# Three edits in one kernel: a copy moved from ScalarE to VectorE in the scan, a stencil by corner sums, softplus by its rounding

## The chip, the cores and the metric

The kernel runs on one core of a Trainium2 chip. The engines of a core run beside each other: TensorE (PE in the profile), VectorE (DVE), ScalarE (ACT), GpSimd (POOL), and SyncE (SP), which issues DMAs. The metric is the device time of one execution in microseconds (us). The kernel before takes 13669.76 us, the median of 3 runs (13667.76 to 13674.38).

## The reference, cut to what matters

The input is `[2, 192, 96, 96]` in float32. Four blocks are added to it in turn, each behind a group norm. Block 1 (two deformable convolutions) and block 3 are not touched. Of blocks 2 and 4 this matters:

```
# block 2: x is the normalised input
lap   = [[0, -1, 0], [-1, 4, -1], [0, -1, 0]]
edges = conv(x, lap)                      # depthwise, padding 1
out   = x + edges                         # 5 x - (up + down + left + right)
y     = conv1x1(out, merge_w) + merge_b   # 192 to 192 channels, then added to the stream

# block 4: tokens t = 0..9215 per image, 384 inner channels, 16 states
delta = softplus(dt_lin + b_dt)
def step(h, inp):
    u_t, d_t, B_t, C_t = inp
    dA = exp(d_t[..., None] * A)
    h = dA * h + (d_t * u_t)[..., None] * B_t[:, None, :]
    y_t = einsum('bdn,bn->bd', h, C_t)
```

## The kernel before, in words

The program is a chain of eight phases, each with its own tiles and semaphores and each closed before the next starts. Three are touched.

**edges_and_merge** (8821.4 to 9144 us of the span) loads an image of 96 x 9216 x 2 halves in four quarters into `X1`. ScalarE writes the normalised image with a border of zeros into `XP` (L963). The image goes through in 48 chunks of 4 rows (384 pixels). For each, GpSimd adds up and down into `T1` (L980) and left and right into `T2` (L981), VectorE adds the two (L1019) and makes `E` = 5 x - sum (L1022), TensorE multiplies by the weights (L992, 4 matmuls in float32, two records each), and VectorE adds bias and residual (L1007) and takes statistics for the next norm (L1012, `bn_stats`). SyncE stores the chunk. The second image is loaded only when the first is through.

**mamba_inputs** (10296 to 11022 us) has 36 steps of 512 tokens. TensorE makes the inner projections in `PX` and `PZ`; ScalarE copies `PX` to `XH` (`fill`, L1681), takes silu, and of the step size v it makes relu(v), |v| and `EE` = exp(-|v|) (L1707 to L1713), and then ln(1 + `EE`) (L1719). VectorE makes the depthwise convolution (L1783, L1788), copies `PD` (L1829), and in `small` and `whole` finishes softplus: below 2^-7 a polynomial of third degree stands for ln(1 + e) (L1798 to L1815).

**mamba_scan** (11022 to 13664 us) has 36 chunks of 512 tokens and 16 states n each, which makes 576 steps i; 384 channels lie on 128 partitions in three groups d. A step runs over four engines:
- ScalarE writes `BU`, four scaled copies of 128x384 (L1960), one for each 128 tokens `tb`, with the scale read from the tile, then three exponentials of 128x512 into `DA` (L1967). It also copies the carry of an earlier step (L1943).
- TensorE transposes `BU` into `PB` in PSUM (`turn`, L2014, once for each d), and adds G of two steps earlier to `PY` by an identity matmul (`accumulate`, L2024).
- VectorE runs `scan(i, d)` (L2072): `tensor_tensor_scan` over 512 tokens, with `DA` in SBUF and `PB` in PSUM as inputs, `HH` in SBUF as output.
- GpSimd multiplies `HH` of the step by row C (`CB`, spread over the partitions by a DMA) into `G`, 128x1536 in one instruction (L1988), once `scan(i, 2)` has ended.

Once a chunk, at n = 2, VectorE does `skip_path` (L2077) and `gate` (L2082) for each d; at n = 4 to 9 TensorE does `project` (L2032), at n = 10 VectorE `put` (L2090) and GpSimd `gain` (L1977); at n = 11 and 12 TensorE does `turn_gain`. `BU`, `DA`, `HH` and `G` have three buffers each. `PB` has one for each d, so that `turn(i + 1, d)` waits for `scan(i, d)`.

The order on each engine is as written in the code; nothing else sets it. `p.tick` is a 1x1 memset that raises a semaphore.

Of the kernel before, what the change touches and what calls it, by code (L numbers as in the profile page):

```python
# [8 lines left out]
ACT = mybir.ActivationFunctionType  # L9
# [4 lines left out]
HW = H * W  # L14
# [9 lines left out]
NEAR1 = 2.0 ** -7  # L24
HC = C // 2
# [872 lines left out]
def edges_and_merge(nc, k):  # L898

    RC = 4  # L900
    NP = RC * W
    NCH = H // RC
    WP = W + 2
    with Phase(nc, "ed") as p:
        GN = p.sb([HC, 4, 2])
        group_norm_terms(nc, k, k.ST, NCH, GN)
        X1 = p.sb([HC, 2, HW])
        XP = p.sb([HC, 2, (H + 2) * WP])
        T1 = p.sb([HC, 2, 2, NP])
        T2 = p.sb([HC, 2, 2, NP])  # L910
        E = p.sb([HC, 2, 2, NP])
        XO = p.sb([HC, 2, 2, NP])
        WM = p.sb([HC, 2, C])
        BM = p.sb([HC, 2])
        PE = [p.ps([HC, 2, 512]) for _ in range(2)]
        s_w, s_v, s_z, s_xn, s_t, s_e, s_pe, s_xo, s_bf, s_tf, s_x1f = p.sems(11)
        s_wr = p.sems(2)
        s_x1 = p.sems(4)
        s_st = p.sems(2)
        QR = H // 4  # L920
        XPv = XP[:, :, :].rearrange("p h (y x) -> p h y x", x=WP)
        chunks = [(c // NCH, c % NCH) for c in range(B * NCH)]

        def at(r, dy, dx, h):
            return XPv[:, h, r * RC + 1 + dy:r * RC + 1 + dy + RC, 1 + dx:1 + dx + W]

        def tile(T, q, h):
            return T[:, q, h, :].rearrange("p (y x) -> p y x", x=W)

        with p.block() as blk:  # L930
            @blk.sync
            def _(e):
                e.dma_start(WM[:, :, :], k.d["w_mergeT"].rearrange("(h p) o -> p h o", p=HC)).then_inc(s_w, 16)
                e.dma_start(BM[:, :], k.d["b_mergeT"]).then_inc(s_w, 16)
                e.wait_ge(s_w, 32).then_inc(s_w, -32)
                for s in s_wr:
                    e.sem_inc(s, 1)
                for b in range(B):
                    if b:
                        e.wait_ge(s_x1f, 1).then_inc(s_x1f, -1)  # L940
                    for i in range(4):
                        n0, n1 = i * QR * W, (i + 1) * QR * W
                        e.dma_start(X1[:, :, n0:n1], k.d["x1"][b, :, :, n0:n1].rearrange("h p n -> p h n"))\
                            .then_inc(s_x1[i], 16)
                    for r in range(NCH):
                        c = b * NCH + r
                        q = c % 2
                        e.wait_ge(s_xo, 1).then_inc(s_xo, -1)
                        e.dma_start(k.d["x2"][b, :, :, r * NP:(r + 1) * NP].rearrange("h p n -> p h n"), XO[:, q, :, :])\
                            .then_inc(s_st[q], 16)  # L950
                for q in range(2):
                    e.wait_ge(s_st[q], 16).then_inc(s_st[q], -16)
# [14 lines left out]

            @blk.gpsimd
            def _(e):
                e.memset(XP[:, :, :], 0.0).then_inc(s_z, 1)  # L970
                for c, (b, r) in enumerate(chunks):
                    q = c % 2
                    if r == 0:
                        e.wait_ge(s_xn, 2).then_inc(s_xn, -2)
                    elif r % (NCH // 4) == NCH // 4 - 1 and r < NCH - 1:
                        e.wait_ge(s_xn, 2).then_inc(s_xn, -2)
                    if c >= 2:
                        e.wait_ge(s_tf, 1).then_inc(s_tf, -1)
                    for h in range(2):
                        e.tensor_tensor(tile(T1, q, h), at(r, -1, 0, h), at(r, 1, 0, h), ALU.add)  # L980
                        ins = e.tensor_tensor(tile(T2, q, h), at(r, 0, -1, h), at(r, 0, 1, h), ALU.add)  # L981
                    ins.then_inc(s_t, 1)

            @blk.tensor
            def _(e):
                e.wait_ge(s_wr[0], 1).then_inc(s_wr[0], -1)
                for c in range(len(chunks)):
                    q = c % 2
                    e.wait_ge(s_e, 1).then_inc(s_e, -1)
# [588 lines left out]
NS = 16  # L1578
# [637 lines left out]
```

## Time and profile before

| | |
|---|---|
| median of 3 runs | 13669.76 us |
| profiled execution | 13666.01 us |
| its span | 13664.2 us |
| granted TensorE clock, mean | 0.954 |
| TensorE busy | 12753.0 us (93%) |
| VectorE busy | 11814.1 us (86%) |
| ScalarE busy | 11116.3 us (81%) |
| GpSimd busy | 7173.1 us (52%) |

The span runs from the first to the last recorded instruction; the profiled execution took 1.8 us more. Times in the rows are microseconds from the span's start, and L12 is a line of the kernel before. An engine's busy time says how much it worked, not that others waited for it; that is told by the brackets of a row of the timeline, `[0.88 <-PE ms_p L2024]`: the engine stood idle for 0.88 us ahead of this instruction, until line 2024 on TensorE was done. `DVEq` stands for the engine's own queue, where a wait on a semaphore is held. PEclk is the granted TensorE clock in tenths: 1.00 is 2.4 GHz, 0.50 is 1.2 GHz. `x9` is a row of nine instructions of one form, back to back.

### The profile page before, as it was taken

The page shows a single profiled execution, that of the slowest core. Times are in us where ns is not written, and L with a number is a line of the kernel's source. Part 1 is how long each engine was busy: PE and PEld are TensorE (multiplying, and loading weights), DVE is VectorE, ACT ScalarE, POOL GpSimd, SP SyncE. Part 2 cuts the span into 40 slices and gives each one's busy share as a digit, 9 for nine tenths or more (in the row PEclk, how much of TensorE's full clock was granted, in tenths as well). Part 3 has the DMA queues.
Part 4 walks back from the last instruction along what each step waited for, and adds up shares of the span by engine and source line. Part 5 has one row for each costly group of instructions (what it writes and reads, how often), then busy time and mean ns, then how long its engine had stood idle before and what let it go on. Part 6 is the DMA issues. An engine that isn't in the chain of part 4 may idle for free. (4 is left out here: it accounts for less than half of the span.)

```text
span 13664.2 us, 237197 instructions
## 1 busy us (share of the span) xinstructions
PE 12753.0 (93%) x80318; PEld 10364.2 (76%) x80318; DVE 11814.1 (86%) x15792; ACT 11116.3 (81%) x13034; POOL 7173.1 (52%) x3803
## 2 busy tenths in 40 slices
PE   7899999999999999999999999866098989999999
PEld 4799999999999999999999999322033345555555
DVE  4699999999999999999999999579867978888888
ACT  2688888888888888888888888219676878998898
POOL 0255555555555555555555555143320058888887
PEclk9999999999999999999999999578598889999999
DMA  4677767667777766767776666734443433333332
GB/s 124 161 178 179 178 178 177 177 177 178 178 179 178 177 177 177 179 177 178 179 177 177 178 177 169 187 82 165 132 133 119 151 116 106 103 105 99 105 103 85
DMA packets 826538, 2102.27 MB, mean 154 GB/s; under 512 B 83476, under 2 KB 440266, under 8 KB 681802
## 3 DMA queue, kind: packets, MB, share of 16 engines
q1 hardware_dynamic: 760994, 2046.19, 56.4%
q10 hardware_dynamic: 64359, 40.89, 1.1%
q8 instruction: 669, 10.96, 0.4%
q14 instruction: 516, 4.22, 0.1%
HBM read 1818.10 MB, written 268.74 MB: 153 GB/s over the span
## 5 line engine op out<-in xcount | busy, mean ns | idle before, releaser
L513 PE MATMUL dc_p<-dc_t 96*128 96x144 f32 x51948 | 6846.2, 285 | 25.8 <-PEq L510 25.8
L579 POOL TENSOR_TENSOR dc_t<-dc_t 128x648 f32<-128x648 f32 x2885 | 4526.3, 1569 | 4016.6 <-POOLq L578 3970.1
L513 PEld LDWEIGHTS dc_p<-dc_t 96*128 96x128 f32 x51948 | 6529.7, 189 | 47.0 <-issue 26.3
L639 DVE TENSOR_TENSOR dc_t<-dc_p,dc_t 128x1296 f32<-128x1296 f32 x2886 | 4343.7, 1505 | 507.3 <-DVEq L637 444.6
L458 ACT ACTIVATE dc_t<-dc_t 96x1152 f32<-96x1152 f32 x2892 | 3590.2, 1241 | 464.0 <-ACTq L482 457.4
L460 ACT ACTIVATE dc_t<-dc_t 96x1152 f32<-96x1152 f32 x2892 | 3367.7, 1164 | 347.2 <-ACTq L459 10.1
L2072 DVE TENSOR_TENSOR_SCAN ms_t<-ms_t,ms_p 128x512 f32<-128x512 f32 x1728 | 2128.4, 1271 | 283.3 <-PE ms_p L2014 203.5
L1988 POOL TENSOR_TENSOR ms_t<-ms_t 128x1536 f32<-128x1536 f32 x576 | 1987.9, 3456 | 503.3 <-DVE ms_t L2072 499.5
L2024 PE MATMUL ms_p<-ms_t,top_t 128*128 128x512 f32 x3456 | 1774.7, 596 | 0.0
L553 PE MATMUL dc_p<-dc_t 128*128 128x180 f32 (+1 forms) x7488 | 1633.6, 318 | 14.7 <-PEq L548 8.7
L2014 PEld LDWEIGHTS ms_p<-top_t,ms_t 128*128 128x128 f32 x6912 | 848.7, 141 | 968.6 <-issue 692.1
L651 DVE TENSOR_TENSOR dc_t<-dc_t 128x648 f32<-128x648 f32 x1442 | 1196.0, 829 | 211.8 <-DVEq L649 197.2
L1960 ACT ACTIVATE ms_t<-ms_t 128x384 f32<-128x384 f32 x2304 | 1222.2, 602 | 24.2 <-PE ms_p L2014 24.1
L553 PEld LDWEIGHTS dc_p<-dc_t 128*128 128x128 f32 (+1 forms) x7488 | 1162.1, 190 | 40.9 <-issue 34.4
L1967 ACT ACTIVATE ms_t<-ms_t 128x512 f32<-128x512 f32 x1728 | 1114.1, 708 | 0.0
L2014 PE MATMUL ms_p<-top_t,ms_t 128*128 128x128 f32 x6912 | 1047.1, 274 | 58.5 <-DVE ms_t L2072 51.6
L629 DVE COPY dc_t<-dc_p 128x128 f32<-128x128 f32 (+1 forms) x3744 | 978.4, 280 | 0.0
L542 PE MATMUL dc_p<-top_t,dc_t 128*128 128x128 f32 (+1 forms) x3744 | 877.8, 272 | 0.5 <-PEq L539 0.5
L659 DVE TENSOR_TENSOR dc_t<-dc_t 128x324 f32<-128x324 f32 x1441 | 703.6, 488 | 0.0
L1977 POOL TENSOR_TENSOR ms_t<-ms_t 128x1536 f32<-128x1536 f32 x36 | 124.6, 3461 | 812.5 <-DMA ms_t<-bcd 812.5
L2024 PEld LDWEIGHTS ms_p<-ms_t,top_t 128*128 128x128 f32 x3456 | 522.2, 191 | 15.8 <-DVE ms_t L2082 11.5
L542 PEld LDWEIGHTS dc_p<-top_t,dc_t 128*128 128x128 f32 (+1 forms) x3744 | 516.9, 138 | 11.9 <-issue 0.7
(209 smaller groups left out, 9823.8 us busy)
## 6 DMA issues: line engine op xcount, KB each, us to landing
dc_t<-sxd SPq DMA_DIRECT2D x1446, 864.0 KB, 5.7
ms_t<-bcd SPq DMA_DIRECT2D x576, 256.0 KB, 3.3
dc_t<-xrT SPq DMA_DIRECT2D x145, 675.0 KB, 8.3
kvd<-wk_t SPq DMA_DIRECT2D x18, 1536.0 KB, 5.1
xvd<-mi_t SPq DMA_DIRECT2D x36, 768.0 KB, 3.5
szd<-mi_t SPq DMA_DIRECT2D x36, 768.0 KB, 5.7
dld<-mi_t SPq DMA_DIRECT2D x36, 768.0 KB, 3.4
ms_t<-dld SPq DMA_DIRECT2D x36, 768.0 KB, 6.8
```

The source lines that it names most:

```text
L458: e.activation(HX[:, q, u, :], HX[:, q, u, :], ACT.Abs, bias=QX[:, 0:1]).then_inc(s_ab, 1)
L460: e.activation(HX[:, q, u, :], HX[:, q, u, :], ACT.Relu, bias=1.0, scale=-1.0).then_inc(s_hx, 1)
L513: ins = e.matmul(PT[j % 2][:, t // 3, (t % 3) * 144:(t % 3 + 1) * 144], HX[:, m // 2 % RP, m % 2, t * 128:(t + 1) * 128], XW[:, i, ky:ky + ...
L542: ins = e.transpose(PR[0:o, u * 128:(u + 1) * 128], VA[:, n // NG % 2, 128 * c:128 * c + o], k.ident[:, :])
L553: ins = e.matmul(PF[:, conv * CM:(conv + 1) * CM], VT[0:o, n % 2, u, :], WD[0:o, c, conv, :], start=(c == 0), stop=(c == NCK - 1), skip_gr ...
L579: e.tensor_tensor(z[:, :, 0:HALF], z[:, :, 0:HALF], z[:, :, HALF:2 * HALF], ALU.add)\
L639: e.tensor_tensor(Zt[:, n % 4, :].rearrange("p (b m i) -> p b m i", b=3, i=CG), PT[n % 2][:, :, 0:432].rearrange("p b (m i) -> p b m i", i ...
L1960: ins = e.activation(BU[:, i % RT, tb, :], UT[:, c % 2, tb, 0:DI], ACT.Copy, scale=UT[:, c % 2, tb, DI + n:DI + n + 1])
L1988: e.tensor_tensor(G[:, i % RG, :, :], HH[:, i % RH, :, :], CB[:, i % RB, :].unsqueeze(1).to_broadcast([128, ND, T]), ALU.mult).then_inc(s_ ...
L2014: ins = e.transpose(PB[:, d, tb * 128:(tb + 1) * 128], BU[:, i % RT, tb, d * 128:(d + 1) * 128], k.ident[:, :])
L2024: e.matmul(PY[:, d, :], k.ident[:, :], G[:, i % RG, d, :], start=(n == 0), stop=(n == NS - 1))\
L2072: e.tensor_tensor_scan(HH[:, i % RH, d, :], DA[:, i % RA, d, :], PB[:, d, :], CAR[:, n, d:d + 1], ALU.mult, ALU.add).then_inc(s_scan, 1)
```

## The change: what it does

**In edges_and_merge** chunks have 8 rows, 24 in all, and come in through a ring of six. The sum down + right of a pixel is the sum up + left of its lower right neighbour: `corner` makes all sums U(y, x) = up + left once (one instruction of 96x1746), `around` adds U(y, x) and U(y + 1, x + 1) (96x1536), `edge` takes it from 5 x (96x1536). GpSimd makes no adds. The residual is added on TensorE, by an identity matmul from `XI`. ScalarE adds the bias (`put`) and issues the stores. The second image follows without a break.

**In mamba_inputs** softplus is relu(v) + ln(EU) - ((EU - 1) - EE) with EU = 1 + EE rounded; the bracket is the rounding of the sum. The polynomial, its clip and one of the two passes in `whole` go; one `tensor_tensor` comes in.

**In mamba_scan** ScalarE makes only three of the four copies of `BU` in odd steps. VectorE makes the fourth in a new function, `last_block(i + 2)`, which stands between `scan(i, 0)` and `scan(i, 1)` of odd steps i.

```diff
 def edges_and_merge(nc, k):
-    RC = 4
+    RC = 8
+    RX, RO = 6, 4
...
+            @blk.tensor
...
+                    e.wait_ge(s_xi[c % RX], 16 * (c // RX + 1))
+                    e.wait_ge(s_e, c + 1)
                     if c >= 2:
+                        e.wait_ge(s_xo, c - 1)
                     for m in range(2):
+                        for j in range(2):
+                            part = slice(j * (NP // 2), (j + 1) * (NP // 2))
+                            out = PE[q][:, 2 * m + j, 0:NP // 2]
+                            e.matmul(out, k.ident[0:HC, 0:HC], XI[:, c % RX, m, part], start=True, stop=False)
+                            for h in range(2):
+                                ins = e.matmul(out, WM[:, h, m * HC:(m + 1) * HC], S[:, q, j * (RC // 2):(j + 1) * (RC // 2), h, :],
+                                               start=False, stop=(h == 1))
...
+                def corner(c):
+                    r = c % NCH
+                    y = r * RC + 1
+                    e.wait_ge(s_xn, c + 1 if r == NCH - 1 else c + 2)
+                    e.tensor_tensor(lines(U[:, c % 2]), lines(XP[:, y - 1:y + RC, :, 1:W + 2]), lines(XP[:, y:y + RC + 1, :, 0:W + 1]),
+                                    ALU.add).then_inc(s_u, 1)
...
+                for c in range(N + 3):
+                    if c < N:
+                        corner(c)
+                    if 1 <= c <= N:
+                        edge(c - 1)
+                    if c < N:
+                        around(c)
+                    if c >= 3:
+                        statistics(c - 3)
...
 def mamba_inputs(nc, k):
...
                     if 1 <= n <= N:
                         e.wait_ge(s_dt, 1).then_inc(s_dt, -1)
-                        e.wait_ge(s_fe, 1).then_inc(s_fe, -1)
...
-                        e.activation(DL[:, q, :, :], EE[:, q, :, :], ACT.Ln, bias=1.0).then_inc(s_ln, 1)
+                        e.activation(DL[:, q, :, :], EU[:, q, :, :], ACT.Ln).then_inc(s_ln, 1)
...
                 def small(n):
...
-                    e.tensor_scalar(ES[:, :, :], EE[:, q, :, :], NEAR1, None, ALU.min).then_inc(s_v, 1)
+                    e.tensor_scalar(EU[:, q, :, :], EE[:, q, :, :], 1.0, None, ALU.add).then_inc(s_v, 1)
                     e.wait_ge(s_v, 1).then_inc(s_v, -1)
-                    e.tensor_scalar(EE[:, q, :, :], EE[:, q, :, :], NEAR1, None, ALU.max).then_inc(s_clip, 1)
-                    e.scalar_tensor_tensor(out=PP[:, q, :, :], in0=ES[:, :, :], scalar=-1.5, in1=ES[:, :, :],
-                                           op0=ALU.add, op1=ALU.mult).then_inc(s_v, 1)
+                    e.scalar_tensor_tensor(out=PP[:, q, :, :], in0=EU[:, q, :, :], scalar=1.0, in1=EE[:, q, :, :],
+                                           op0=ALU.subtract, op1=ALU.subtract).then_inc(s_v, 1)
                     e.wait_ge(s_v, 1).then_inc(s_v, -1)
-                    e.scalar_tensor_tensor(out=PP[:, q, :, :], in0=PP[:, q, :, :], scalar=3.0, in1=ES[:, :, :],
-                                           op0=ALU.add, op1=ALU.mult).then_inc(s_v, 1)
-                    e.wait_ge(s_v, 1).then_inc(s_v, -1)
+                    e.tensor_tensor(PP[:, q, :, :], XS[:, n % 3, :, :], PP[:, q, :, :], ALU.subtract).then_inc(s_clip, 1)
...
                     e.scalar_tensor_tensor(out=DL[:, q, :, :], in0=DL[:, q, :, :], scalar=LT[:, 0:1],
-                                           in1=XS[:, n % 3, :, :], op0=ALU.subtract, op1=ALU.add).then_inc(s_v, 1)
-                    e.wait_ge(s_v, 1).then_inc(s_v, -1)
-                    p.tick(e, s_fe)
-                    e.scalar_tensor_tensor(out=DL[:, q, :, :], in0=PP[:, q, :, :], scalar=1.0 / 3.0,
-                                           in1=DL[:, q, :, :], op0=ALU.mult, op1=ALU.add).then_inc(s_so, 1)
+                                           in1=PP[:, q, :, :], op0=ALU.subtract, op1=ALU.add).then_inc(s_so, 1)
...
 def mamba_scan(nc, k):
...
-                    for tb in range(TB):
+                    for tb in range(TB - i % 2):
...
                     if d == 0:
                         e.wait_ge(s_ba, i + 1)
+                        if i % 2:
+                            e.wait_ge(s_bd, i // 2 + 1)
...
+                def last_block(i):
+                    c, n = i // NS, i % NS
+                    e.wait_ge(s_ev, TB * (c + 1))
+                    if i >= RT:
+                        e.wait_ge(s_db, ND * (i - RT + 1))
+                    e.tensor_scalar(BU[:, i % RT, TB - 1, :], UT[:, c % 2, TB - 1, 0:DI],
+                                    UT[:, c % 2, TB - 1, DI + n:DI + n + 1], None, ALU.mult).then_inc(s_bd, 1)
...
+                last_block(1)
                 for i in range(N + NS):
                     c, n = i // NS, i % NS
                     for d in range(ND):
+                        if d == 1 and i % 2 and i + 2 < N:
+                            last_block(i + 2)
```

The order of instructions on an engine is shown below in the program's order. VectorE in mamba_scan before, around the n = 2 of a chunk; `ms_t` is any SBUF tile of the phase, `ms_p` any PSUM tile, L2072 is the scan:

```order
L2072 SCALAR_TENSOR_TENSOR ms_t<-ms_t,ms_p 128x512 x54
L2077 SCALAR_TENSOR_TENSOR ms_p<-ms_t,ms_p 128x512
L2072 SCALAR_TENSOR_TENSOR ms_t<-ms_t,ms_p 128x512
L2082 TENSOR_TENSOR ms_t<-ms_p,ms_t 128x512
L2077 SCALAR_TENSOR_TENSOR ms_p<-ms_t,ms_p 128x512
```

And now, where L2083 is the scan, L2096 `skip_path`, L2101 `gate` and L2091 `last_block`:

```order
L2083 SCALAR_TENSOR_TENSOR ms_t<-ms_t,ms_p 128x512 x6
L2091 TENSOR_SCALAR ms_t<-ms_t 128x384
L2083 SCALAR_TENSOR_TENSOR ms_t<-ms_t,ms_p 128x512 x2
L2096 SCALAR_TENSOR_TENSOR ms_p<-ms_t,ms_p 128x512
L2083 SCALAR_TENSOR_TENSOR ms_t<-ms_t,ms_p 128x512
L2101 TENSOR_TENSOR ms_t<-ms_p,ms_t 128x512
```

After every sixth scan, the first of an odd step, stands one `last_block`; n = 2 is an even step and has none. TensorE in edges_and_merge before, where L992 is the weight matmul:

```order
L992 MATMUL ed_p<-ed_t 96x384 x192
```

And now, where L997 is the identity matmul with the input (`top_t` is the identity) and L999 the weight matmul:

```order
L997 MATMUL ed_p<-ed_t,top_t 96x384
L999 MATMUL ed_p<-ed_t 96x384 x2
L997 MATMUL ed_p<-ed_t,top_t 96x384
L999 MATMUL ed_p<-ed_t 96x384 x2
```

There are 288 matmuls in place of 192, all of 384 columns.

There are no reordered instructions in mamba_inputs: of a step's six passes of VectorE over 128x1536 four are left, and one memset is gone.

## Rows read from the trace of the kernel before

**Rows 1.** Busy time by stretch: us, busy us and instructions of each engine, PEclk, DMA share, GB/s.
```profile
8600.00:8800.00 200.00, 200.00 (x314) 88.70 (x313) 121.79 (x234) 48.52 (x75) 0.00 (x0) 0.50 0.88 215
...
8850.00:8984.00 134.00, 100.38 (x192) 41.71 (x192) 123.51 (x215) 9.03 (x4) 85.84 (x89) 0.73 0.22 61
...
9930.00:10270.00 340.00, 322.76 (x736) 117.69 (x734) 220.88 (x186) 267.60 (x305) 63.42 (x27) 0.99 0.45 128
...
11045.00:13664.00 2619.00, 2554.07 (x11354) 1455.60 (x11352) 2295.24 (x1980) 2351.08 (x4739) 2106.04 (x611) 1.00 0.33 99
```

**Rows 2.** The scan in order of time: start us, us, engine, line, form [idle before, releaser].
```profile
11480.27 0.75 DVE L2077 SCALAR_TENSOR_TENSOR ms_p<-ms_t,ms_p 128x512 f32<-128x512 f32 x1 [0.88 <-PE ms_p L2024]
...
11487.56 10.64 DVE L2072 TENSOR_TENSOR_SCAN ms_t<-ms_t,ms_p 128x512 f32<-128x512 f32 x9
...
11548.01 3.46 POOL L1988 TENSOR_TENSOR ms_t<-ms_t 128x1536 f32<-128x1536 f32 x1 [0.43 <-DVE ms_t L2072]
...
11548.09 3.73 DVE L2072 TENSOR_TENSOR_SCAN ms_t<-ms_t,ms_p 128x512 f32<-128x512 f32 x3 [0.16 <-ACT ms_t L1967]
...
11551.90 3.46 POOL L1988 TENSOR_TENSOR ms_t<-ms_t 128x1536 f32<-128x1536 f32 x1 [0.43 <-DVE ms_t L2072]
...
11552.70 0.75 DVE L2077 SCALAR_TENSOR_TENSOR ms_p<-ms_t,ms_p 128x512 f32<-128x512 f32 x1 [0.88 <-PE ms_p L2024]
...
11557.12 0.66 PE L2014 MATMUL ms_p<-top_t,ms_t 128*128 128x128 f32 x4 [0.57 <-DVE ms_t L2072]
```

**Rows 3.** VectorE and GpSimd together, in edges_and_merge and in wkv, in order of time.
```profile
8970.07 2.31 DVE L1019 TENSOR_TENSOR ed_t<-ed_t 96x384 f32<-96x384 f32 x2
...
8970.82 1.14 POOL L981 TENSOR_TENSOR ed_t<-ed_t 96x384 f32<-96x384 f32 x1
...
8975.97 1.00 DVE L1019 TENSOR_TENSOR ed_t<-ed_t 96x384 f32<-96x384 f32 x2
...
9300.55 3.44 POOL L1268 TENSOR_TENSOR wk_t<-wk_t 128x1536 f32<-128x1536 f32 x1 [1.47 <-issue]
...
9302.75 2.85 DVE L1311 TENSOR_TENSOR wk_t<-wk_t 128x1536 f32<-128x1536 f32 x1
...
9312.59 1.76 DVE L1297 TENSOR_TENSOR wk_t<-wk_t 128x1536 f32<-128x1536 f32 x1
```

**Rows 4.** VectorE's groups by form: line, form, count | busy us, mean ns | idle.
```profile
L1783 DVE TENSOR_SCALAR mi_t<-mi_t 128x512 f32<-128x512 f32 x108 | 52.6, 544 | 20.3 <-DVEq L1781 19.0
...
L1798 DVE TENSOR_SCALAR mi_t<-mi_t 128x1536 f32<-128x1536 f32 x36 | 34.1, 948 | 7.8 <-DVEq L1797 7.8
```

**Rows 5.** edges_and_merge in order of time: start, first loads of weights, the phase's end.
```profile
8837.69 9.03 ACT L963 ACTIVATE ed_t<-ed_t 96x2304 f32<-96x2304 f32 x4 [17.21 <-ACTq L961]
...
8851.61 0.28 PEld L992 LDWEIGHTS ed_p<-ed_t 96*96 96x96 f32 x1 [0.36 <-issue]
...
8852.25 0.28 PEld L992 LDWEIGHTS ed_p<-ed_t 96*96 96x96 f32 x1 [0.36 <-issue]
...
8855.32 0.16 PEld L992 LDWEIGHTS ed_p<-ed_t 96*96 96x96 f32 x1 [0.22 <-issue]
...
8855.64 0.16 PEld L992 LDWEIGHTS ed_p<-ed_t 96*96 96x96 f32 x1 [0.16 <-issue]
...
9144.24 2.79 DVE L96 BATCH_NORM_AGGREGATE gn_t<-top_t 96x2 f32<-96x144 f32 x4 [3.02 <-PEq L930]
```

**Rows 6.** mamba_inputs in order of time: ScalarE fill (L1681), VectorE copy (L1829), the tail.
```profile
10347.60 1.45 ACT L1681 ACTIVATE mi_t<-mi_p 128x1536 f32<-128x1536 f32 x1 [2.24 <-ACTq L1680]
...
10617.41 0.68 DVE L1829 COPY mi_t<-mi_p 44x512 f32<-44x512 f32 x1
...
10635.98 0.68 DVE L1829 COPY mi_t<-mi_p 44x512 f32<-44x512 f32 x1
...
10675.17 1.45 ACT L1681 ACTIVATE mi_t<-mi_p 128x1536 f32<-128x1536 f32 x1 [0.34 <-ACTq L1680]
...
10971.78 3.75 PE L1749 MATMUL mi_p<-mi_t 12*128 12x512 f32 x4 [4.36 <-PEq L1747]
```

More of the change, by code:

```diff
@@ L898, in edges_and_merge, with lines @@
 def edges_and_merge(nc, k):
-    RC = 4
+    RC = 8
     NP = RC * W
     NCH = H // RC
+    N = B * NCH
     WP = W + 2
+    RX, RO = 6, 4
     with Phase(nc, "ed") as p:
         GN = p.sb([HC, 4, 2])
[L906 to L912, printed above, removed]
+        group_norm_terms(nc, k, k.ST, 24, GN)
+        XI = p.sb([HC, RX, 2, NP])
+        XP = p.sb([HC, H + 2, 2, WP])
+        U = p.sb([HC, 2, RC + 1, 2, W + 1])
+        S = p.sb([HC, 2, RC, 2, W])
+        XO = p.sb([HC, RO, 2, NP])
         WM = p.sb([HC, 2, C])
         BM = p.sb([HC, 2])
[L915 to L928, printed above, removed]
+        PE = [p.ps([HC, 4, 512]) for _ in range(2)]
+        s_w, s_z, s_xn, s_u, s_s, s_e, s_pe, s_xo, s_bn = p.sems(9)
+        s_xi = p.sems(RX)
+        s_st = p.sems(RO)
+        def lines(t):
+            return t.rearrange("p y h x -> p (y h) x")
         with p.block() as blk:
@@ L951, in _ @@
-                for q in range(2):
-                    e.wait_ge(s_st[q], 16).then_inc(s_st[q], -16)
+                for c in range(N):
+                    b, r = c // NCH, c % NCH
+                    if c >= RX:
+                        e.wait_ge(s_pe, c - RX + 1)
+                    e.dma_start(XI[:, c % RX, :, :], k.d["x1"][b, :, :, r * NP:(r + 1) * NP].rearrange("h p n -> p h n"))\
+                        .then_inc(s_xi[c % RX], 16)
+            @blk.gpsimd
+            def _(e):
+                for edge in (XP[:, 0, :, :], XP[:, H + 1, :, :], XP[:, 1:H + 1, :, 0:1],
+                             XP[:, 1:H + 1, :, W + 1:W + 2]):
+                    e.memset(edge, 0.0).then_inc(s_z, 1)
@@ L968, in _ @@
[L968 to L978, printed above, removed]
-                    for h in range(2):
-                        e.tensor_tensor(tile(T1, q, h), at(r, -1, 0, h), at(r, 1, 0, h), ALU.add)
-                        ins = e.tensor_tensor(tile(T2, q, h), at(r, 0, -1, h), at(r, 0, 1, h), ALU.add)
-                    ins.then_inc(s_t, 1)
+                        e.wait_ge(s_e, c - NCH + 2)
@@ new lines, in store @@
+                def store(c):
+                    b, r, q = c // NCH, c % NCH, c % RO
+                    e.wait_ge(s_xo, c + 1)
+                    e.dma_start(k.d["x2"][b, :, :, r * NP:(r + 1) * NP].rearrange("h p n -> p h n"), XO[:, q, :, :])\
+                        .then_inc(s_st[q], 16)
+                e.wait_ge(s_w, 32)
+                for c in range(3):
+                    affine(c)
+                for c in range(N):
+                    if c + 3 < N:
+                        affine(c + 3)
+                    put(c)
+                    if c >= 1:
+                        store(c - 1)
@@ L984, in _ @@
+                store(N - 1)
+                for q in range(RO):
+                    e.wait_ge(s_st[q], 16 * (N // RO))
             @blk.tensor
             def _(e):
[L986 to L987 removed]
+                e.wait_ge(s_w, 32)
+                for c in range(N):
                     q = c % 2
[L989 removed]
+                    e.wait_ge(s_xi[c % RX], 16 * (c // RX + 1))
+                    e.wait_ge(s_e, c + 1)
+                    if c >= 2:
+                        e.wait_ge(s_xo, c - 1)
@@ new lines, in statistics @@
+                def statistics(c):
+                    b, r = c // NCH, c % NCH
+                    e.wait_ge(s_xo, c + 1)
+                    for m in range(2):
+                        for j in range(2):
+                            ins = e.bn_stats(k.ST[:, 2 * b + m, 2 * r + j, :],
+                                             XO[:, c % RO, m, j * (NP // 2):(j + 1) * (NP // 2)])
+                    ins.then_inc(s_bn, 1)
+                e.wait_ge(s_z, 4)
+                for c in range(N + 3):
[7 more added lines that the diff above has]
+                        statistics(c - 3)
@@ new lines, in edges_and_merge, with _ @@
+        with p.block() as blk:
+            @blk.sync
+            def _(e):
+                for s, total in ((s_w, 32), (s_z, 4), (s_xn, N), (s_u, N), (s_s, N), (s_e, N), (s_pe, N), (s_xo, N), (s_bn, N)):
+                    e.wait_ge(s, total).then_inc(s, -total)
+                for q in range(RX):
+                    e.wait_ge(s_xi[q], 16 * (N // RX)).then_inc(s_xi[q], -16 * (N // RX))
+                for q in range(RO):
+                    e.wait_ge(s_st[q], 16 * (N // RO)).then_inc(s_st[q], -16 * (N // RO))
```

103 lines of the change are left out of this document (32 added, 71 removed).

## The prediction

> **What bounds the kernel now.** I read the busy time by stretch first, since the three edits lie in three closed phases. In the scan TensorE is busy 2554 of 2619 us at PEclk 1.00, ScalarE 2351, VectorE 2295, GpSimd 2106 [rows 1]. The timeline then says who waits: VectorE stands 0.88 us idle for TensorE ahead of a chunk's first `skip_path`; TensorE waits 0.57 us for VectorE once it has fallen behind at n = 2, where VectorE does `skip_path` and `gate` besides the scans [rows 2]. So TensorE leads, and the same instruction comes again after 11552.70 - 11480.27 = 72.43 us: one chunk of 16 steps [rows 2]. A plain step lasts 11551.90 - 11548.01 = 3.89 us, from one multiply of GpSimd to the next [rows 2]; 16 of them are 62.2, and the 10.2 us that are left are `project`, `turn_gain` and the wait at n = 2. VectorE's nine scans back to back take 10.64 us; of one scan 3.73 / 3 or 1.27, so they start every (10.64 - 1.27) / 8 = 1.17 us, three in 3.51. VectorE has 0.38 us to spare in a plain step. GpSimd starts its multiply as `scan(i, 2)` ends and runs 3.46 us, nearly the whole next step [rows 2].
>
> In edges_and_merge VectorE is busy 123.5 of 134 us, with GpSimd at 85.8 and the clock at 0.73 [rows 1]. Mamba_inputs starts its `fill` 18 times in 10675.17 - 10347.60 us, 18.20 each, where a step of VectorE is 18.57 [rows 6]: TensorE with ScalarE and VectorE stand close together.
>
> **The scan.** ScalarE loses one copy in two steps. It was no bound, so that brings nothing. VectorE gains 287 `tensor_scalar` of 128x384. Their own time I bound by rows 4: 0.24 us by elements from 1536 in 0.95, 0.54 by the 512 with two scalars from a tile; I take 0.42, nearer to the second, which has the overhead. By that alone VectorE would need 6 x 1.17 + 0.42 = 7.44 us for two steps against TensorE's 7.8, and the edit would cost nothing.
>
> The wait is what matters. Where VectorE starts an instruction with two SBUF inputs while GpSimd works, it ends only after GpSimd: GpSimd's 3.44 us end at 9303.99, VectorE's pass takes 2.85 instead of 1.76 us and ends at 9305.60, which is GpSimd's end plus 1.61, its own time less 0.15. In edges_and_merge two adds take 2.31 us beside GpSimd and 1.00 alone [rows 3]. The scan of before escapes, because one input lies in PSUM: 3.73 us for three beside 3.46 of GpSimd [rows 2]. `last_block` has one SBUF input only, but `tensor_scalar` takes 0.95 us for 1536 elements where a `tensor_tensor` takes 1.76 [rows 3, 4]: it reads two elements in the time of one. I take it that the second comes by the way in that a second input uses, and so waits the same.
>
> The Trainium skill ("SBUF — State Buffer", section "Who interferes with whom") says that VectorE and GpSimd share one pair of ports, that an instruction in a two-port mode holds it from issue to end while the other is fully blocked, and that `tensor_scalar` can enter such a mode; "VectorE: DVE Perf Modes", section "The perf-mode tier table (the rule you actually need)", has float32 `tensor_scalar` in SBUF at 2x and `tensor_tensor` at 1x. The trace agrees for the rate and for two inputs; it does not show a `tensor_scalar` beside GpSimd. By the rule that an instruction with one SBUF input does not contend, taken alone, the cost would be nil, which is the first rival.
>
> Now two steps, counted from the end of the even step's third scan. GpSimd starts at 0.08 and holds until 3.54. `scan(i, 0)` runs, and at 1.17 `last_block` is issued and stays behind GpSimd; it ends at 3.54 + (0.42 - 0.15) = 3.81. Behind it on VectorE is `scan(i, 1)`, and behind that TensorE, whose `turn(i + 1, 1)` needs that scan's `PB` back. Scans then end 1.27 after 3.70, and four more at 1.17: 9.65 us for two steps, where TensorE needs 7.8, and with `project` up to 2 x (3.89 + 0.9) = 9.6, the 0.9 an estimate from the 10.2 us above; so VectorE becomes the bound almost everywhere. A chunk: 8 x 9.65 = 77.2; at n = 2 three times `skip_path` and `gate`, which with its scan make 2.43 us each (11487.56 - 11480.27 = 7.29 for three [rows 2]) in place of 1.17, +3.8; `put` 1.1, an estimate for 96x1024 from 1.76 us for 1536 in rows 3. Sum 82.1 against 72.4: +9.7, and over 35.6 chunks +345 us. Bounds: 0 if nothing waits (not below, since TensorE's work stays what it is and fills 97% of the stretch); +280 if 0.2 us of each blocked pair are saved, since the multiply may start later than 0.08 when it waits for TensorE (0.23 x 8 x 36 = 65); +470 if in one step of a chunk it waits for `gain` as well, which is as long as the multiply, 3.46 x 36 = 125. I take 345.
>
> **Edges.** TensorE gets 24 records of 384 columns for a chunk of 8 rows, where it had 16. A record (TensorE keeps two for a float32 matmul) is 0.32 us at full clock and 0.64 at half, by the starts of the loads at 8855.32, 8855.64 and 8851.61, 8852.25 [rows 5]: 7.7 us a chunk. VectorE, free of GpSimd, needs 1746/1536 x 1.76 + 2 x 1.76 = 5.5 and four `bn_stats` of some 0.5 by the same rate: 7.5, hidden under TensorE. ScalarE's share, some 4 us, is hidden too. So 24 x 7.73 = 186 us. Start: ScalarE waited 17.2 us for its first quarter [rows 5]; a third of it is there some 10 us sooner, at 8828, and two or three passes of ScalarE and three of VectorE follow, so TensorE starts at 8840 (an estimate); half clock at first +4, last `put` and statistics +4, the closing block, now with a reset of every semaphore, +6. The next phase's first instruction comes at 9040 in place of 9144.24 [rows 5]: -104 us. The clock decides: if it stays at half, 24 x 24 x 0.64 = 369 us. Against that stands the stretch from 9930, in gate_and_project, where TensorE runs at 0.99, busy 95% of the time; for it the one from 8600, at 0.50 though TensorE is busy all 200 us [rows 1]. Bounds -110 and +80.
>
> **Softplus.** A step of VectorE loses a pass at 0.95, one at 1.76 and some 0.2 of waits and the memset: 18.57 - 2.9 = 15.7 us. The ring through TensorE and ScalarE is 18.20 and is now the bound; that gives back 0.37 in some 15 steps, 5.7 us. At the end TensorE's 4.36 us wait for VectorE's copy [rows 6] goes, and two finishing pairs are a pass shorter: 7 us. Sum -13 us, between -5 and -25, should the ring itself have been held by VectorE now and then.
>
> **Sum.** 13666.0 - 104 - 13 + 345 = 13894 us in the profiled execution. The median lies 3.8 above that execution: 13898, and I say 13895.
>
> **Rivals.**
> 1. *`last_block` does not wait for GpSimd*, having one SBUF input. Then its 0.42 us lie in the 0.76 us that VectorE has to spare in two plain steps, and the scan keeps its 72.4 us. Time 13666 + 4 - 117 = 13553: faster. For it: no row of before shows a single-input instruction held by GpSimd. Against: the double rate. It decides from a block of under 0.1 us. 0.13.
> 2. *As forecast, and TensorE stays at half clock in edges_and_merge*: 369 instead of 186 us, 13895 + 183 = 14078. For it the stretch at 8600, against it the one at 9930. 0.05.
> 3. *VectorE is held for only part of GpSimd's instruction*, half of the 2.4 us: +170 in place of 345, 13720. For it: rounds of GpSimd's work might let VectorE in between; against it rows 3, where the end is GpSimd's end to 0.05 us. 0.04.
>
> The forecast itself has 0.78; its own range is 13,830 to 13,960. The range of 8 in 10 is 13,780 to 14,010: it takes in the bounds of the scan but for the far ends. Faster by over 0.2% (27 us, about what can be told from no change here) is rival 1 with a grain of rival 3: 0.14. Within 0.2%: 0.02. Slower: 0.84.
>
> **What would show it.** In the scan's timeline, a `tensor_scalar` of 128x384 of some 2.6 us from issue to end, ending with GpSimd's multiply plus 0.3; VectorE without idle time, TensorE waiting for the scan with some 9 us a chunk, 82 us from one `skip_path` to the next; ScalarE's three copies bring nothing. In edges_and_merge PEclk near 1.0 and loads 0.32 apart, the next group norm at 9040. In mamba_inputs VectorE idle 2 us a step. Wrong it would be if `last_block` took 0.4 us beside a running multiply, or if PEclk stayed at 0.5 in edges_and_merge.

## The result, and the profile after

The changed kernel takes 13849.82 us, the median of 4 runs (13843.18 to 13852.75), against 13669.28 before in the same comparison: ratio 1.0131, interval 1.0113 to 1.0148. Slower by 1.3%, with 13895 forecast. The profiled execution took 13843.18 us with a span of 13841.4. Cut at the same VectorE instruction at the start of each phase, the two spans differ by +177.2 us as follows:

| phase | before | after | difference | forecast |
|---|---|---|---|---|
| up to the end of edges_and_merge's norm | 8820.96 | 8818.91 | -2.1 | 0 |
| edges_and_merge | 323.28 | 216.11 | -107.2 | -104 |
| wkv, gate_and_project | 1144.79 | 1144.02 | -0.8 | 0 |
| mamba_inputs | 734.01 | 714.17 | -19.8 | -13 |
| mamba_scan | 2641.16 | 2948.19 | +307.0 | +345 |

**The scan.** First the groups by form of the kernel after (line, engine, form, count, busy us, mean ns, idle before):

```profile
L1997 POOL TENSOR_TENSOR ms_t<-ms_t 128x1536 f32<-128x1536 f32 x576 | 1993.1, 3466 | 804.0 <-DVE ms_t L2083 794.7
...
L2083 DVE TENSOR_TENSOR_SCAN ms_t<-ms_t,ms_p 128x512 f32<-128x512 f32 x1728 | 2072.6, 1255 | 4.7 <-ACT ms_t L1976 3.6
...
L2091 DVE TENSOR_SCALAR ms_t<-ms_t 128x384 f32<-128x384 f32 x288 | 719.5, 2498 | 18.5 <-ACT ms_t L1945 18.5
```

`last_block` (L2091) takes 2498 ns on the mean. Its timeline, with GpSimd's multiply (L1997), the scan (L2083) and `skip_path` (L2096); start, us, engine, line, [idle before, releaser]:

```profile
11164.78 0.72 DVE L2096 SCALAR_TENSOR_TENSOR ms_p<-ms_t,ms_p 128x512 f32<-128x512 f32 x1
...
11245.60 0.73 DVE L2096 SCALAR_TENSOR_TENSOR ms_p<-ms_t,ms_p 128x512 f32<-128x512 f32 x1
...
11414.05 3.46 POOL L1997 TENSOR_TENSOR ms_t<-ms_t 128x1536 f32<-128x1536 f32 x1 [3.22 <-DVE ms_t L2083]
...
11415.66 2.06 DVE L2091 TENSOR_SCALAR ms_t<-ms_t 128x384 f32<-128x384 f32 x1
...
11418.97 0.66 PE L2025 MATMUL ms_p<-top_t,ms_t 128*128 128x128 f32 x4 [1.59 <-DVE ms_t L2083]
...
11577.26 2.07 DVE L2091 TENSOR_SCALAR ms_t<-ms_t 128x384 f32<-128x384 f32 x1
...
11586.29 2.66 DVE L2091 TENSOR_SCALAR ms_t<-ms_t 128x384 f32<-128x384 f32 x1
...
11588.88 7.13 DVE L2083 TENSOR_TENSOR_SCAN ms_t<-ms_t,ms_p 128x512 f32<-128x512 f32 x6
...
11595.92 2.66 DVE L2091 TENSOR_SCALAR ms_t<-ms_t 128x384 f32<-128x384 f32 x1
...
11614.07 3.45 POOL L1986 TENSOR_TENSOR ms_t<-ms_t 128x1536 f32<-128x1536 f32 x1
...
11616.31 1.42 DVE L2091 TENSOR_SCALAR ms_t<-ms_t 128x384 f32<-128x384 f32 x1
...
11624.84 3.21 DVE L2091 TENSOR_SCALAR ms_t<-ms_t 128x384 f32<-128x384 f32 x1
```

The second `last_block` here is the clearest: GpSimd's multiply runs from 11414.05 to 11417.51; `last_block` starts at 11415.66 and ends at 11417.72, 0.21 us behind GpSimd. TensorE then waits 1.59 us for the scan that stood behind it, where [rows 2] had 0.57. The pair of steps is 11595.92 - 11586.29 = 9.63 us, and from one `skip_path` to the next it is 11245.60 - 11164.78 = 80.82 us, where [rows 2] had 72.43. VectorE has no idle time ahead of `skip_path` any more.

All 287 blocks of this trace that stand in the scan start inside a GpSimd instruction, and each ends 0.21 to 0.22 us behind it. Three of the eight blocks of a chunk differ from the 2.66 us of the others: 2.07 after n = 2, where `gate` stands between GpSimd's start and the block, so that less of the multiply is left; 1.42 at n = 11, which meets the end of `gain` (L1986, 11614.07 to 11617.52, the block ends at 11617.73); 3.21 at n = 13, since GpSimd, late by `gain`, has a multiply just begun when the block is issued.

Busy time by stretch after (us, busy us and instructions of PE, PEld, DVE, ACT, POOL, PEclk, DMA share, GB/s), edges_and_merge and the scan:

```profile
8850.00:9030.00 180.00, 177.07 (x550) 89.10 (x548) 157.76 (x160) 76.40 (x87) 0.00 (x0) 1.00 0.43 135
...
10893.00:13841.00 2948.00, 2627.31 (x11376) 1438.57 (x11376) 2907.30 (x2269) 2246.79 (x4461) 2114.20 (x612) 0.99 0.31 91
```

In the scan VectorE is busy 2907 of 2948 us: it is the bound now. ScalarE fell to 2247 and nothing came of it. In edges_and_merge PEclk is 1.00, against 0.73 in [rows 1].

**Edges.** TensorE's first matmul, loads of weights within a chunk, ScalarE's `put` and VectorE's `around`:

```profile
8837.72 1.57 PE L997 MATMUL ed_p<-ed_t,top_t 96*96 96x384 f32 x2 [21.19 <-DVE ed_t L1022]
...
8900.81 0.16 PEld L997 LDWEIGHTS ed_p<-ed_t,top_t 96*96 96x96 f32 x1 [0.16 <-issue]
...
8901.14 0.16 PEld L997 LDWEIGHTS ed_p<-ed_t,top_t 96*96 96x96 f32 x1 [0.16 <-issue]
...
8903.27 0.90 ACT L961 ACTIVATE ed_t<-ed_p,ed_t 96x768 f32<-96x768 f32 x1 [4.21 <-PE ed_p L999]
...
8903.34 1.75 DVE L1016 TENSOR_TENSOR ed_t<-ed_t 96x1536 f32<-96x1536 f32 x1 [0.59 <-PE ed_p L999]
```

```profile
9035.02 2.79 DVE L95 BATCH_NORM_AGGREGATE gn_t<-top_t 96x2 f32<-96x144 f32 x4 [4.26 <-PEq L1045]
```

Loads stand 0.33 us apart, `around` waits 0.59 us for TensorE, and the next norm starts at 9035.02: the order of events that was forecast, TensorE in the lead.

**Softplus.** ScalarE's `fill` twice and VectorE's convolution in the kernel after:

```profile
10488.83 1.45 ACT L1700 ACTIVATE mi_t<-mi_p 128x1536 f32<-128x1536 f32 x1 [0.96 <-ACTq L1699]
...
10506.11 1.45 ACT L1700 ACTIVATE mi_t<-mi_p 128x1536 f32<-128x1536 f32 x1 [0.96 <-ACTq L1699]
```

```profile
10507.83 1.46 DVE L1800 TENSOR_SCALAR mi_t<-mi_t 128x512 f32<-128x512 f32 x3 [2.05 <-DVEq L1798]
```

VectorE waits 2.05 us a step for ScalarE's `fill`; the forecast said 2. A turn of the ring, from one `fill` to the next, is 17.28 us here, and elsewhere in the phase 17.66 or 19.27. Busy time and PEclk of one turn of each length (columns as above):

```profile
10364.75:10384.02 19.27, 19.27 (x37) 6.72 (x37) 14.50 (x19) 14.80 (x15) 0.00 (x0) 0.82 0.50 168
...
10401.69:10419.35 17.66, 17.66 (x37) 6.46 (x37) 14.50 (x19) 14.80 (x15) 0.00 (x0) 0.90 0.48 160
...
10488.83:10506.11 17.28, 16.01 (x37) 6.15 (x37) 14.49 (x19) 14.80 (x15) 0.00 (x0) 1.00 0.49 165
```

VectorE and ScalarE do the same work in all three; what differs is the granted clock. At a mean of 0.82 and 0.90 TensorE is busy for the whole turn, at 1.00 for 16.01 of 17.28 us.

### The profile page after: what moved, and what is told of

It reads as the page before. It is cut to its first block and busy times, and to the rows that moved or that the text cites. A ratio compares the mean times of both kernels' runs of the same rounds, so it can differ in the third digit from the quotient of the medians.

```text
span 13841.4 us, 236977 instructions
## 1 busy us (share of the span) xinstructions
PE 12797.4 (92%) x80510; PEld 10355.1 (75%) x80510; DVE 12243.0 (88%) x15708; ACT 11054.2 (80%) x12826; POOL 6971.6 (50%) x3614
## 5 line engine op out<-in xcount | busy, mean ns | idle before, releaser
L1997 POOL TENSOR_TENSOR ms_t<-ms_t 128x1536 f32<-128x1536 f32 x576 | 1993.1, 3466 | 804.0 <-DVE ms_t L2083 794.7
L2083 DVE TENSOR_TENSOR_SCAN ms_t<-ms_t,ms_p 128x512 f32<-128x512 f32 x1728 | 2072.6, 1255 | 4.7 <-ACT ms_t L1976 3.6
L1969 ACT ACTIVATE ms_t<-ms_t 128x384 f32<-128x384 f32 x2016 | 1075.6, 601 | 2.3
L2091 DVE TENSOR_SCALAR ms_t<-ms_t 128x384 f32<-128x384 f32 x288 | 719.5, 2498 | 18.5 <-ACT ms_t L1945 18.5
```

What stands on the lines that cost most here:

```text
L1997: e.tensor_tensor(G[:, i % RG, :, :], HH[:, i % RH, :, :], CB[:, i % RB, :].unsqueeze(1).to_broadcast([128, ND, T]), ALU.mult).then_inc(s_ ...
L2083: e.tensor_tensor_scan(HH[:, i % RH, d, :], DA[:, i % RA, d, :], PB[:, d, :], CAR[:, n, d:d + 1], ALU.mult, ALU.add).then_inc(s_scan, 1)
```

## The experiments

**1. The scan as before** (the whole of the change but `last_block`).

```diff
-                    for tb in range(TB - i % 2):
+                    for tb in range(TB):
```
and `last_block` with its semaphore left out.

> The changed kernel with mamba_scan as before: ScalarE makes all four copies in every step. Theory A (VectorE's tensor_scalar is held until GpSimd's multiply ends, and that is the whole loss): a chunk of the scan is back at 72.43 us from 80.8, the scan 307 us shorter, and 13850 - 307 = 13543 us. Theory B (part of the loss comes from the other two edits, for instance data that the scan reads later): the scan stays above 2641 us from its first VectorE instruction to the end, and the time above 13600.

Measured 13537.78 us (ratio to before 0.9903, interval 0.9886 to 0.9919); a chunk is 11568.70 - 11496.26 = 72.44 us. Theory A holds for the chunks: the other two edits cost them nothing. The phase as a whole took 2645.2 us, 303.0 less than in the changed kernel but 4.0 more than before, which is above the 2641 of theory B, though its time above 13600 did not come. These 4 us lie ahead of the first and behind the last `skip_path`; what makes them is not shown.

**2. `last_block` alone** on the kernel before.

```diff
-def mamba_scan(nc, k):   # before
+def mamba_scan(nc, k):   # of the changed kernel
```

> The kernel before with the new mamba_scan alone. Theory A: 13669 + 307 = 13976 us, chunk 80.8 us. Theory B (the edits act on each other): a chunk other than 80.8, and a time that is off 13976 by more than 20 us.

Measured 13972.78 us (1.0222, 1.0205 to 1.0239), a chunk 80.80 us. The price of 303 us is the edit's own: here too the scan phase is 303.8 us longer than before.

**3. Other rate, same place.**

```diff
+        BL = p.sb([128, RT, ND, 129])
...
-                    e.tensor_scalar(BU[:, i % RT, TB - 1, :], UT[:, c % 2, TB - 1, 0:DI],
+                    e.tensor_scalar(BL[:, i % RT, :, 0:128], UT[:, c % 2, TB - 1, 0:DI].rearrange("p (d t) -> p d t", d=ND),
```

> The changed kernel, but last_block writes to a tile of its own whose rows of 128 elements stand 129 apart, so that input (384 in a row) and output (3 times 128) have different shapes; same place, same engine, same number of elements. TensorE reads that tile. The first last_block, ahead of the scan, runs without GpSimd beside it and tells the rate: 0.42 us is double rate, about 0.6 us single. Theory A: if the rate is single, last_block takes 0.6 us beside GpSimd too, VectorE needs 7.6 us for two steps, a chunk 72.4 to 73.5 us and the time is 13543 to 13585 us; if it stays double, nothing changes, 13850 us. Rival E (any VectorE instruction whose input and output are both in SBUF waits for GpSimd, whatever its rate): single rate, and still 2.8 us beside GpSimd, 13850 to 13900 us.

Measured 13550.07 us (0.9913, 0.9897 to 0.9930). The first `last_block`, alone, and one beside a multiply:

```profile
10913.94 0.61 DVE L2094 TENSOR_SCALAR ms_t<-ms_t 128x384 f32<-128x384 f32 x1 [18.62 <-ACT ms_t L1946]
...
11559.74 3.46 POOL L1998 TENSOR_TENSOR ms_t<-ms_t 128x1536 f32<-128x1536 f32 x1 [1.35 <-DVE ms_t L2086]
...
11560.98 0.59 DVE L2094 TENSOR_SCALAR ms_t<-ms_t 128x384 f32<-128x384 f32 x1
```

All of them, then (count, ns min/median/max):

```profile
L2094 DVE TENSOR_SCALAR ms_t<-ms_t x288: 578/587/615, 10913.9 to 13515.7; 128x384 f32<-128x384 f32 x144
```

Alone it takes 0.61 us instead of 0.42: single rate. Beside the multiply it starts 1.24 us behind GpSimd's start and takes 0.59; none of the 288 takes over 0.615. The same operation on the same number of elements, on the same engine and at the same place of the program, reads and writes SBUF and does not wait for GpSimd once it does not run at double rate. Rival E is out. This is the experiment that carries the cause. The blocks are not quite free: a chunk is 72.77 us, 0.33 more than in experiment 1, which is the 12 us between the two times.

The edit also gives the block a tile of its own, and no run has that tile at double rate. Against the tile as the cause speaks experiment 4, where the block writes the old tile at double rate and takes 0.40 us when it comes first. That one SBUF input does not wait is seen in the kernel before as well: `bn_stats` in edges_and_merge (L1012) reads one SBUF tile and takes 0.54 to 0.56 us each time, though most of the 96 start while an add of GpSimd is running.

```profile
L1012 DVE BATCH_NORM_STATS2 top_t<-ed_t x96: 537/548/558, 8857.2 to 9140.7; 96x6 f32<-96x384 f32 x96
```

**4. Who is first.**

```diff
-                        if d == 1 and i % 2 and i + 2 < N:
+                        if d == 0 and i % 2 and i + 2 < N:
```

> The changed kernel, but last_block(i + 2) stands ahead of scan(i, 0) instead of between scan(i, 0) and scan(i, 1): VectorE comes to it about 0.1 us before GpSimd starts its multiply. Theory A with 'who starts first holds the way in': last_block takes 0.42 us, GpSimd's multiply grows by 0.3 to 0.4 us in odd steps, VectorE needs 7.44 us for two steps against TensorE's 7.8, a chunk takes 72.4 to 73 us, and the time is 13543 to 13565 us. Rival C (VectorE always loses to GpSimd, whoever is first): last_block takes about 3.8 us, worse than the 2.66 of now, a chunk over 88 us and 14100 us or more. Rival D (the price is that of one more instruction with a wait in VectorE's chain, wherever it stands): a chunk stays at 80.8 us and 13850 us.

Measured 13756.9 us (1.0061, 1.0044 to 1.0078): neither of the times that were expected. The timeline shows why. One block that comes first, the one after n = 2, and the one at n = 11, with PEclk 0.50 in the six microseconds behind the second:

```profile
11538.30 0.40 DVE L2091 TENSOR_SCALAR ms_t<-ms_t 128x384 f32<-128x384 f32 x1
...
11538.46 3.55 POOL L1997 TENSOR_TENSOR ms_t<-ms_t 128x1536 f32<-128x1536 f32 x1 [0.44 <-DVE ms_t L2083]
...
11550.03 3.44 POOL L1997 TENSOR_TENSOR ms_t<-ms_t 128x1536 f32<-128x1536 f32 x1 [4.22 <-DVE ms_t L2083]
...
11550.44 3.25 DVE L2091 TENSOR_SCALAR ms_t<-ms_t 128x384 f32<-128x384 f32 x1
...
11555.03 1.09 PE L2025 MATMUL ms_p<-top_t,ms_t 128*128 128x128 f32 x4 [3.31 <-DVE ms_t L2083]
...
11555.91 1.92 PE L2035 MATMUL ms_p<-ms_t,top_t 128*128 128x512 f32 x2
...
11588.86 3.46 POOL L1986 TENSOR_TENSOR ms_t<-ms_t 128x1536 f32<-128x1536 f32 x1
...
11591.70 0.84 DVE L2091 TENSOR_SCALAR ms_t<-ms_t 128x384 f32<-128x384 f32 x1
```

```profile
11555.00:11561.00 6.00, 5.97 (x17) 3.72 (x18) 4.68 (x4) 2.04 (x4) 3.44 (x1) 0.50 0.96 283
```

At 11538.30 VectorE is first: 0.40 us at double rate, and GpSimd's multiply, which starts 0.16 later, grows to 3.55 us. The 0.3 to 0.4 us that were expected for that growth are not met: it is 0.09, since the two overlap for 0.24 us only. Six blocks of a chunk go so, and not seven, as the expectation of experiment 5 below says: the block at n = 11 starts inside `gain` (L1986), takes 0.84 us and ends 0.22 behind it. Rival C is out. After n = 2, though, GpSimd is released by `scan(2, 2)` while VectorE still has the last `gate` to do; the block is issued 0.41 us behind GpSimd and takes 3.25. TensorE stands idle 3.31 us, and its four transposes then take 1.09 us and its two matmuls 1.92, in place of 0.66 and 1.02: half clock, for some 6 us. A chunk is 78.5 us, which is not rival D's 80.8 either.

**5. The same without that one block.**

```diff
-                    for tb in range(TB - i % 2):
+                    for tb in range(TB - (i % 2 and i % NS != 5)):
```
and `last_block` only where i % NS != 3.

> As ahead_of_scan, but in the steps with n = 5 ScalarE makes all four copies, so that there is no last_block right after the gates of n = 2. In ahead_of_scan that one block of a chunk was issued 0.4 us after GpSimd's start, took 3.25 us, and TensorE, idle for 3.31 us behind it, came back at half clock for some 6 us; the other seven took 0.40 us. Theory A (who starts first holds the way in, and one lost race of a chunk makes the whole loss of 6.1 us): no block over 0.8 us, a chunk 72.4 to 72.9 us, 13538 to 13556 us. Rival D (the block has a price wherever it stands): seven eighths of the loss of ahead_of_scan stay, 13730 us.

```profile
L2091 DVE TENSOR_SCALAR ms_t<-ms_t 128x384 f32<-128x384 f32 x252 | 118.9, 472 | 18.8 <-ACT ms_t L1945 18.8
```

Measured 13544.08 us (0.9905, 0.9889 to 0.9922), blocks of 472 ns on the mean, a chunk 72.43 us. So the one lost race made the whole 6.1 us of a chunk. An estimate from the rows of experiment 4: some 3 us are the wait, and 6 us at half clock make up for the other 3. The block at n = 11 still takes 0.84 us, against theory A's "no block over 0.8", and costs nothing. And the block is free to the chunk when it comes first, which is rival D's end. Against experiment 1 it gains nothing either: ScalarE's copy was not on the path.

**6. A shorter multiply.**

```diff
-                    e.tensor_tensor(G[:, i % RG, :, :], HH[:, i % RH, :, :],
+                    e.tensor_tensor(G[:, i % RG, 0:2, :], HH[:, i % RH, 0:2, :],
```

> The changed kernel with GpSimd's multiply over two of the three channel groups (the third keeps zeros, so a third of y is left out). last_block stays where it is. Theory A: the multiply takes 2.3 us in place of 3.46, and last_block 2.66 - 1.15 = 1.5 us. A pair of steps without project takes 8.5 us in place of 9.63, a pair with project is bound by TensorE at 9.5; a chunk 80.8 - 5 x 1.15 - 3 x 0.13 = 74.7 us, 13850 - 36 x 6.1 = 13630 us. Rival F (last_block's length has nothing to do with the multiply's): it stays at 2.66 us and the time at 13850 us.

```profile
11469.76 2.36 POOL L1998 TENSOR_TENSOR ms_t<-ms_t 128x1024 f32<-128x1024 f32 x1 [1.15 <-DVE ms_t L2084]
...
11470.78 1.56 DVE L2092 TENSOR_SCALAR ms_t<-ms_t 128x384 f32<-128x384 f32 x1
```

Measured 13608.66 us, one run. The block ends 0.22 us behind the multiply again; it is shorter as the multiply is shorter. A chunk is 74.12 us, with 74.7 expected. On the mean the block is 1.33 us and not 1.5, because two of the eight meet the multiply later: 0.97 us after n = 2, behind `gate`, and 0.78 at n = 9, where VectorE waits 0.68 us for TensorE ahead of the scan before it. The others take 1.35 to 1.58.

**7 and 8. Edges alone, softplus alone** on the kernel before.

```diff
-def edges_and_merge(nc, k):   # before; in 8: mamba_inputs
+def edges_and_merge(nc, k):   # of the changed kernel; in 8: mamba_inputs
```

> The kernel before with the new edges_and_merge alone. Theory A: the phase takes 216 us in place of 323, and 13670 - 107 = 13563 us. Rival: the gain is partly lost behind the phase (weights of the next phase, a colder clock); over 13575 us.

> The kernel before with the new mamba_inputs alone. Theory A: as in the changed kernel's trace the phase is 20 us shorter: 13650 us. Rival: only the 13 us of the prediction belong to it, and the rest is from another phase: 13657 us.

Edges: 13560.88 us (0.9922, 0.9905 to 0.9938), the phase 215.67 us. Theory A. Softplus: 13652.15 us, median of 10 runs (0.9987, 0.9977 to 0.9996), so between 5 and 31 us less; that leaves both 13 and 20 open. In its trace the phase took 721.4 us, 12.6 less than before; in the changed kernel's 19.8.

The traces of the other experiments settle it, since each has one of the two versions of mamba_inputs. The old one took 733.4 to 734.0 us in three traces. The new one took 719.8 to 721.6 in six, which is 12 to 14 less, and 714.2, 716.1 and 716.6 in three (the changed kernel, experiments 3 and 6). These three are the ones with four to six turns of 17.28 us, at full clock; the others have one at most. So the edit gives some 13 us, and up to 6 more come from the clock of that execution.

**9. Edges without the residual.**

```diff
-                            e.matmul(out, k.ident[0:HC, 0:HC], XI[:, c % RX, m, part], start=True, stop=False)
```
and the first weight matmul starts the sum in its place. Here and in experiment 10 `last_block` is left out too, as in experiment 1.

> The kernel no_last_block (13538 us) with the identity matmuls of edges_and_merge left out, so the residual is missing. Theory G (TensorE bounds the new phase at 24 records of 0.32 us a chunk): VectorE takes over as the bound with 1.96 + 1.75 + 1.75 + 1.93 less overlaps, about 7.1 us a chunk in place of 7.73; the phase is 24 x 0.6 = 14 us shorter, 13524 us. Rival H (VectorE already bounds it): no change.

```profile
8904.75 1.75 DVE L1014 TENSOR_TENSOR ed_t<-ed_t 96x1536 f32<-96x1536 f32 x1
...
8904.92 5.37 PE L997 MATMUL ed_p<-ed_t 96*96 96x384 f32 x16 [1.69 <-issue]
...
8911.81 1.75 DVE L1014 TENSOR_TENSOR ed_t<-ed_t 96x1536 f32<-96x1536 f32 x1
```

The total, 13534.14 us of one run, says little, since in that execution edges_and_merge began 13.7 us later than in experiment 1. The phase itself took 195.82 us in place of 214.54, 18.7 less where 14 were expected. A chunk is 8911.81 - 8904.75 = 7.06 us, VectorE without a gap and TensorE idle 1.69 us: theory G. TensorE bounds the new phase, with VectorE 0.67 us behind it.

**10. The corner sums on GpSimd.**

```diff
-                    if c < N:
-                        corner(c)
```
and the same `tensor_tensor` in GpSimd's queue.

> The kernel no_last_block with the corner sums made by GpSimd in place of VectorE. GpSimd needs some 3.9 us for 1746 elements, by 3.46 us for 1536. Theory A: edge and around have two SBUF inputs and wait for it; the three share one way in, 3.9 + 1.75 + 1.75 = 7.4 us a chunk at best and, where an instruction of VectorE starts just behind GpSimd's, up to 4 us longer for it: rows of edge or around above 3 us, a chunk 7.8 to 9.5 us, and the phase 0 to 45 us longer. Rival J (the waits come only from reading the same tile): rows of edge (XP, S) that GpSimd does not write stay at 1.75 us, VectorE has 2 us to spare a chunk, and the phase keeps its 216 us.

```profile
8900.70 3.89 POOL L947 TENSOR_TENSOR ed_t<-ed_t 96x1746 f32<-96x1746 f32 x1 [3.86 <-ACT ed_t L958]
...
8901.90 4.31 DVE L1024 SCALAR_TENSOR_TENSOR ed_t<-ed_t 96x1536 f32<-96x1536 f32 x1
...
8910.14 1.74 DVE L1024 SCALAR_TENSOR_TENSOR ed_t<-ed_t 96x1536 f32<-96x1536 f32 x1
...
8910.15 5.48 POOL L947 TENSOR_TENSOR ed_t<-ed_t 96x1746 f32<-96x1746 f32 x1 [5.56 <-ACT ed_t L958]
```

Measured 13569.19 us, one run, the phase 240.64 us, 26.1 more. `edge`, whose tiles GpSimd does not write, takes 4.31 us when it starts inside GpSimd's instruction, which ends at 8904.59 and the pass at 8906.21, 1.62 later. That rules out rival J's forecast of 1.75 us for it. Both read `XP`, though, so this run alone does not separate a shared tile from a shared way in; the scan does, where `last_block` (`UT` to `BU`) and the multiply (`HH` and `CB` to `G`) have no tile in common.

At 8910.14 the race goes the other way. `edge` starts 0.01 us ahead of GpSimd and takes its own 1.74; GpSimd's instruction takes 5.48 us in place of 3.89, longer by 1.59, where the two overlap for 1.73. So whoever comes second is held, GpSimd as much as VectorE. Experiment 4 fits this: an overlap of 0.24 us there, and a growth of 0.09, which is in both cases the overlap less 0.14 or 0.15.

## Why the prediction was right

The sign, the mechanism and the time were right; three sizes were off. In the profiled execution 13894 us were forecast and 13843 measured; the misses all go the same way (38 us in the scan, 7 in mamba_inputs, 3 in edges_and_merge, 3 elsewhere), so none hid another.

- *`last_block` waits for GpSimd.* Right, by experiments 1 to 6. The forecast had 2.6 us for the block, ending with GpSimd's multiply plus 0.3; measured 2.66 and 0.21. The pair of steps was 9.65 forecast and 9.63 measured. The step from "two SBUF inputs" in [rows 3] to "double rate" was an inference there and is shown by experiment 3. The 0.42 us for the block alone was a pick between 0.24 and 0.54 and came out to the digit by luck; it matters little, since a held block costs mainly what is left of the multiply.
- *Rival 1*, no wait, is out; what it gave for the time, 13553, is what the kernel takes when the wait is taken away by other means: 13550 in experiment 3, 13544 in experiment 5, 13538 in experiment 1 without the block.
- *Rival 3*, a partial hold, is out: the block ends 0.21 or 0.22 us behind GpSimd's instruction, whatever its length. What that rival quotes from [rows 3], an end "to 0.05 us" at GpSimd's, stands in no row: the pass there ends 1.61 us behind GpSimd.
- *+345 for the scan* was mis-sized: 307, of which 303 are the block's (experiments 1 and 2) and 4.0 stand in the kernel without it too. The term is the chunk of 82.1 us, in which all eight blocks were priced alike. Measured 80.8: the block after n = 2 is 0.6 us shorter, that at n = 11 1.2 shorter, that at n = 13 0.6 longer, together -1.3 a chunk, -46 us in 36. The bound of +470, a second wait behind `gain`, did not come: `gain` stands behind the multiply of n = 9 and leaves the block of n = 11 only its end to wait for.
- *Edges, -104*: -107.2. TensorE started at 8837.7 instead of 8840. *Rival 2*, half clock in that phase, did not come: 1.00 from 8850 on, with TensorE busy 177 of 180 us.
- *Softplus, -13*: -19.8 in this trace. The tail gave the 7 us forecast: from the last `fill` to the scan it was 69.1 us and is 62.0. The ring gave 13 where 5.7 was forecast. It was taken as fixed at 18.20, which is the mean of the turns 17.66, 17.66 and 19.27 that follow one another in most of the phase; in this execution six turns at full clock took 17.28 instead, 5.5 us together. In the five traces of the new version without such a turn (experiments 4, 5, 8, 9 and 10) the last `fill` comes 631.0 to 632.4 us behind the first, where the old version has 637.9 to 638.1: the forecast's 6 us. So the mechanism and the 13 us held, and the rest of the 19.8 is the clock; why it stayed full for these turns is not shown.

## What to carry to other kernels

Before work is moved to VectorE while GpSimd runs long instructions, look at how the new instruction reads: a float32 `tensor_scalar` from SBUF to SBUF at double rate is held until GpSimd's instruction ends, and so costs not its own 0.42 us but what is left of GpSimd's 3.46. It is not held when it is issued first, or when it runs at single rate (0.59 us, at 0.33 us a chunk here). But the one that is first holds the other: with two SBUF inputs and 1.74 us on VectorE, GpSimd's instruction took 1.59 us longer in experiment 10. And nothing is won by taking work off an engine that is not on the path: of 0.6 us of ScalarE in every second step nothing came back in any of the variants; the kernel to keep is that of experiment 1, 13538 us.

## What the runs showed of the hardware that had not been expected

- One wait of 3.31 us on TensorE cost twice: it came back at half clock, with transposes at 1.09 us for four instead of 0.66, and a chunk lost 6.1 us for a block of 3.25.
- A `tensor_scalar` whose output rows are 129 elements apart, with 128 used, went at single rate (0.61 us for 384 elements instead of 0.42).
- Where VectorE is first, GpSimd is held in its turn, for the time of the overlap less some 0.15 us: 3.55 us instead of 3.46 behind a block of 0.40, and 5.48 instead of 3.89 behind a pass of 1.74 that started 0.01 us ahead of it.
- A turn of the ring in mamba_inputs took 17.28, 17.66 or 19.27 us with the same instructions, at a mean granted clock of 1.00, 0.90 and 0.82. The mix differed between executions, and with it the phase: 714.2 to 721.6 us for the same code in nine traces.
